# Top-2 expert layer in a fused six-layer kernel: first tile's rows picked on TensorE, last two tiles placed by TensorE

## The reference, cut to what matters

```python
x = x + _L1_attn_ref(_layernorm(x, axis=-1), ...)
x = x + _L1_ffn_ref(_layernorm(x, axis=-1), Wg, w1, w3, w2)

def _L1_ffn_ref(hidden_states, Wg, w1, w3, w2):      # 8 experts, top 2, hidden 256, inter 704
    router_logits = x @ Wg.T
    probs = jax.nn.softmax(router_logits, axis=-1)
    topk_vals, topk_idx = jax.lax.top_k(probs, TOP_K)
    topk_vals = topk_vals / jnp.sum(topk_vals, axis=-1, keepdims=True)
    combine = jnp.zeros((T, NUM_EXPERTS)).at[jnp.arange(T)[:, None], topk_idx].add(topk_vals)
    for e in range(NUM_EXPERTS):
        h = jax.nn.silu(x @ w1[e].T) * (x @ w3[e].T)
        out = out + combine[:, e:e + 1] * (h @ w2[e].T)
```

## Time and profile before

| what | value |
|---|---|
| median of 3 runs | 807.28 us |
| profiled execution, its own time | 807.86 us |
| profiled execution, span from first to last instruction | 806.0 us |
| TensorE busy | 737.7 us, 92% |
| VectorE busy | 563.9 us, 70% |
| ScalarE busy | 414.3 us, 51% |
| GpSimd busy | 310.5 us, 39% |
| largest entry of the chain that ended last | scatters into `sums_d`, 11% |
| mean granted TensorE clock | 0.91 |

### The profile page before, as it was taken

One profiled execution on the slowest core, in us unless ns is written; L12 is line 12 of the kernel. 1 busy time (PEld: TensorE's weight loads), 2 busy tenths in 40 slices (PEclk: granted clock), 3 DMA queues, 4 the chain that ended last, 5 costly groups with the idle time before them and its releaser, 6 DMA issues.

```text
span 806.0 us, 15830 instructions
## 1 busy us (share of the span) xinstructions
PE 737.7 (92%) x5985; PEld 585.5 (73%) x5985; DVE 563.9 (70%) x870; ACT 414.3 (51%) x892; POOL 310.5 (39%) x346
## 2 busy tenths in 40 slices
PE   7888999899999989979988899999889988999995
PEld 6623333678888767867865699986678865999995
DVE  5998997578887857777988566646588745655453
ACT  2877888335544434534455566653345540544542
POOL 2078888413332234433475113212133212232341
PEclk8855555799999999999999999999999999999999
DMA  6089999202211113311111011011011235999952
GB/s 191 26 147 160 173 167 181 66 14 78 75 61 57 44 39 93 91 53 38 48 55 52 14 34 53 28 47 66 27 54 41 86 119 193 395 390 380 325 136 69
DMA packets 110649, 87.92 MB, mean 109 GB/s; under 512 B 71313, under 2 KB 92177, under 8 KB 110578
## 3 DMA queue, kind: packets, MB, share of 16 engines
q1 hardware_dynamic: 107842, 83.16, 36.5%
q0 software_dynamic: 2736, 3.80, 2.5%
HBM read 66.62 MB, written 3.54 MB: 87 GB/s over the span
## 4 chain that ended last, share of the span: by engine, by line
PE 46%; DVE 17%; DMA 14%; POOL 9%; issue 7%; ACT 5%; DVEq 1%; SPq 0%; POOLq 0%; ACTq 0%
DMA sums_d<-og,scatter_idx 11%; PE ps L198 10%; PE ps L200 8%; PE ps L199 8%; POOL pt L856 6%; PE ps L1718 4%; PE ps L2101 2%; DVE x L1485 2%; PE ps L1188 2%; PE ps L1698 2%; DVE qrot L2273 2%; PE ps L2418 2%; POOL nb L863 2%; PE ps L1199 1%; ACT soft L2234 1%
## 5 line engine op out<-in xcount | busy, mean ns | idle before, releaser
L330 POOL TENSOR_TENSOR wa_lo<-raw,wa_hi 128x256 fp32r<-128x256 f32 (+1 forms) x76 | 85.6, 1131 | 184.9 <-ACT wa_hi L319 184.5
L330 POOL TENSOR_TENSOR wb_lo<-raw,wb_hi 128x256 fp32r<-128x256 f32 (+1 forms) x68 | 61.6, 911 | 129.4 <-ACT wb_hi L319 129.4
L959 ACT ACTIVATE kres<-ps,nb,qs 128x1024 int16<-128x1024 f32 x64 | 77.1, 1204 | 17.7 <-POOL nb L863 16.6
L2418 PE MATMUL ps<-xgt,tw 128*128 128x128 f32 x720 | 84.6, 278 | 1.4 <-ACT xgt L2484 1.4
L1092 DVE TENSOR_REDUCE nm<-ps 128x1 f32<-128x1024 f32 x64 | 78.0, 1222 | 9.8 <-PE ps L782 7.4
L2418 PEld LDWEIGHTS ps<-xgt,tw 128*128 128x128 f32 x720 | 83.2, 195 | 2.1 <-ACT xgt L2484 2.1
L198 PE MATMUL ps<-xt_hi,wa_hi 128*128 128x512 f32 (+1 forms) x168 | 68.5, 408 | 1.7 <-DVE soft L1343 0.9
L782 PE MATMUL ps<-qkt 48*128 48x512 bf16 x128 | 65.5, 617 | 4.9 <-ACT kres L959 3.8
L856 POOL CAST pt<-pti 128x1024 bf16<-128x1024 int16 x62 | 64.3, 1037 | 5.4 <-DMA pti<-kres 2.0
L199 PE MATMUL ps<-xt_lo,wa_hi 128*128 128x512 f32 (+1 forms) x168 | 65.0, 387 | 0.0
L200 PE MATMUL ps<-xt_hi,wa_lo 128*128 128x512 f32 (+1 forms) x168 | 64.9, 386 | 0.0
(11 more groups left out here) (414 smaller groups left out, 1941.7 us busy)
## 6 DMA issues: line engine op xcount, KB each, us to landing
tw<-w_l1f SPq DMA_DIRECT2D x15, 2304.0 KB, 13.9
raw<-w_l0a SPq DMA_DIRECT2D x16, 256.0 KB, 3.0
raw<-w_l1p SPq DMA_DIRECT2D x32, 128.0 KB, 2.1
raw<-w_l1x SPq DMA_DIRECT2D x32, 128.0 KB, 2.1
raw<-w_l1a SPq DMA_DIRECT2D x16, 256.0 KB, 2.6
raw<-w_l0f SPq DMA_DIRECT2D x12, 256.0 KB, 2.8
raw<-w_l0a SPq DMA_DIRECT2D x16, 128.0 KB, 2.1
wv_raw<-w_l0a SPq DMA_DIRECT2D x8, 256.0 KB, 3.2
```

Of the source, the lines that this page charges most:

```text
L330: last = nc.gpsimd.tensor_tensor(split_lo, src, split_hi.bitcast(F32), ALU.subtract)
L959: nc.scalar.activation(ei[:, n % RING, :], slot(n), ACT.Exp, bias=nb[:, n % 3:n % 3 + 1], scale=qs[:, col:col + 1], accum_out=sums[:, u, k ...
L2418: last = nc.tensor.matmul(up_gate(m, g)[:, k * P:(k + 1) * P], tw[:, slot_of_tile(m), k, (2 * g + c) * P:(2 * g + c + 1) * P], xgt[:, u, c ...
```

## The change

Three things are done in one edit.

1. **First tile.** Tile 0's rows are no longer gathered. VectorE builds `first_at`, a one-hot table of the tokens whose first-choice place (`own_i[:, 0:NT]`, the lower of a token's two places) lies in rows 0 to 127, and TensorE multiplies `xn` with it (8 float32 matmuls), which gives the transposed rows at once. The gathers are those of tiles 1 to 14, two of them before `scatter_idx` is awaited.
2. **Expert table.** `begun`, `begun_sum`, `expert_of` stand right after `first_at`, ahead of `own_tile`, `own_row` and the `place_j` tables. The weights by slot (`slot_weights`) are moved behind `up(0)` on TensorE and behind the first product on VectorE. Of the dummy matmuls twelve and two go, one is added.
3. **Last two tiles.** Tiles 13 and 14 are both placed by one-hot matmuls (8 tables `last_at`); their rows are split into `og_hi` (ScalarE) and `og_lo` (VectorE). The sums are loaded back after the scatter of tile 12. Tile 14's gate and product are made in two halves, and its down product is 6 float32 matmuls straight from `hx` and `tw` without the split.

```diff
+PLACED = TILES - 2
@@ tiles_sync
-            sp.wait_ge(added, 16 * LAST)
+            sp.wait_ge(added, 16 * PLACED)
@@ l1f_pe
             busy(pe, 2, 8)
+            pe.wait_ge(mo["first_at"], mo_at("first_at", 1))
+            for c in range(C2):
+                for t in range(NT):
+                    last = nc.tensor.matmul(ps[:, 4, c * P:(c + 1) * P], xn[:, t, c * P:(c + 1) * P], first_at[:, t, :], start=t == 0, stop=t == NT - 1)
+            last.then_inc(mo["x_t"], 1)
             pe.wait_ge(mo["token_v"], mo_at("token_v", 1))
...
-            busy(pe, 2, 12)
-            pe.wait_ge(mo["weight_v"], mo_at("weight_v", 1))
-            for j in range(8):
-                last = nc.tensor.matmul(ps[:, 7, 0:2 * SLOTS], place_j[:, j, :], weight_v[:, j, :], start=j == 0, stop=j == 7)
-            last.then_inc(mo["weights"], 1)
...
                         for c in range(C2):
                             last = nc.tensor.matmul(up_gate(m, g)[:, k * P:(k + 1) * P], tw[:, slot_of_tile(m), k, (2 * g + c) * P:(2 * g + c + 1) * P], xgt[:, u, c, :], start=c == 0, stop=c == 1)
+                        if m == LAST and g == 1 and k == 1:
+                            last.then_inc(mo["up"], 1)
...
-            gathered(0)
-            busy(pe, 2, 2)
+            busy(pe, 2, 1)
             for m in range(TILES + 1):
                 if m < TILES:
                     up(m)
+                if m == 0:
+                    slot_weights()
                 if m + 1 < TILES:
                     gathered(m + 1)
-                if m:
+                if m and m < TILES:
                     down(m - 1)
+            down_last(pe)
+            rows_placed(pe, PLACED)
+            rows_placed(pe, LAST)
+
+        def down_last(pe):
+            for i, k in enumerate((3, 4, 5, 0, 1, 2)):
+                if i % 3 == 0:
+                    pe.wait_ge(mo["h"], mo_at("h", TILES + i // 3))
+                last = nc.tensor.matmul(ps[:, 6, 0:D], hx[:, k * P:(k + 1) * P], tw[:, slot_of_tile(LAST), k, 4 * P:6 * P], start=i == 0, stop=i == CHUNKS - 1)
+            last.then_inc(mo["down"], 1)
@@ l1f_pool
-            for m in range(3):
+            for m in range(1, 3):
                 gather(m)
             pool.wait_ge(mo["scatter_at"], mo_at("scatter_at", 1))
-            for m in range(LAST + 2):
+            for m in range(PLACED + 2):
@@ l1f_act
-                h_high(m)
-                if m + 1 < TILES:
+                if m < LAST:
+                    h_high(m)
+                if m + 1 < LAST:
                     down_high(m + 1)
+            for m in (PLACED, LAST):
+                act.wait_ge(mo["down"], mo_at("down", m + 1))
+                nc.scalar.activation(og_hi[:, m - PLACED, :], ps[:, 7 if m < LAST else 6, 0:D], ACT.Copy, scale=slot_w[:, m:m + 1]).then_inc(mo["row_hi"], 1)
@@ l1f_dve
+            nc.vector.tensor_tensor(first_at[:], count_j[:].unsqueeze(1).broadcast_to([P, NT, P]), own_i[:, 0:NT].unsqueeze(2).broadcast_to([P, NT, P]), ALU.is_equal).then_inc(mo["first_at"], 1)
...
+                if m == LAST:
+                    dve.wait_ge(mo["up"], mo_at("up", TILES + 1))
+                    for k in range(2):
+                        cols = slice(3 * P * (1 - k), 3 * P * (2 - k))
+                        dve.wait_ge(mo["gate"], mo_at("gate", TILES + k))
+                        nc.vector.tensor_tensor(hx[:, cols], act_g[:, m % 2, cols], up_gate(m, 1)[:, cols], ALU.mult).then_inc(mo["h"], 1)
+                    return
...
+                if m >= PLACED:
+                    dve.wait_ge(mo["row_hi"], mo_at("row_hi", m - PLACED + 1))
+                    nc.vector.scalar_tensor_tensor(og_lo[:, m - PLACED, :], ps[:, 7 if m < LAST else 6, 0:D], slot_w[:, m:m + 1], og_hi[:, m - PLACED, :].bitcast(F32), ALU.mult, ALU.subtract).then_inc(mo["scaled"], 1)
+                    return
```

More of the change, by code:

```diff
@@ L549, in build @@
         masks = sb("masks", [P, 2, SLOTS], ctx=m5)
-        last_id = sb("last_id", [P, 1], ctx=m5)
-        last_at = sb("last_at", [P, NT, P], ctx=m5)
+        first_at = sb("first_at", [P, NT, P], ctx=m5)
+        last_id = sb("last_id", [P, 2], ctx=m5)
+        last_at = sb("last_at", [P, 2, NT, P], F32R, m5)
+        og_hi = sb("og_hi", [P, 2, D], F32R, m5)
+        og_lo = sb("og_lo", [P, 2, D], F32R, m5)
         logit = sb("logit", [P, NT, 16], ctx=m5)
@@ L2564, in l1f_dve @@
             dve.wait_ge(step, c.up())
+            nc.vector.tensor_tensor(first_at[:], count_j[:].unsqueeze(1).broadcast_to([P, NT, P]), own_i[:, 0:NT].unsqueeze(2).broadcast_to([P, NT, P]), ALU.is_equal).then_inc(mo["first_at"], 1)
+            dve.wait_ge(mo["ranks"], mo_at("ranks", 2))
+            dve.wait_ge(mo["table"], mo_at("table", 11))
+            nc.vector.tensor_tensor(begun[:], ps[:, 5, 0:8].unsqueeze(1).broadcast_to([P, SLOTS, 8]), tile_at[:].unsqueeze(2).broadcast_to([P, SLOTS, 8]), ALU.is_le).then_inc(step, 1)
+            dve.wait_ge(step, c.up())
+            nc.vector.tensor_reduce(begun_sum[:], begun[:], AX.X, ALU.add).then_inc(step, 1)
+            dve.wait_ge(step, c.up())
+            nc.vector.tensor_scalar(expert_of[:], begun_sum[:], -1.0, None, ALU.add).then_inc(mo["expert"], 1)
             nc.vector.tensor_scalar(own_tile[:], own_i[:], 7, None, ALU.arith_shift_right).then_inc(step, 1)
@@ L2578, in l1f_dve @@
             places(1)
[L2579 to L2585, removed]
             dve.wait_ge(mo["tokens"], mo_at("tokens", 1))
@@ L2646, in last_places, with slot_weights @@
                 dve.wait_ge(mo["scatter_at"], mo_at("scatter_at", 1))
-                nc.vector.tensor_copy(last_id[:], scatter_idx[:, LAST:TILES]).then_inc(step, 1)
+                nc.vector.tensor_copy(last_id[:], scatter_idx[:, PLACED:TILES]).then_inc(step, 1)
                 dve.wait_ge(step, c.up())
-                for t in range(NT):
-                    nc.vector.tensor_scalar(last_at[:, t, :], count_j[:], float(t * P), last_id[:, 0:1], ALU.add, ALU.is_equal).then_inc(mo["last_at"], 1)
+                for i in range(2):
+                    for t in range(NT):
+                        nc.vector.tensor_scalar(last_at[:, i, t, :], count_j[:], float(t * P), last_id[:, i:i + 1], ALU.add, ALU.is_equal).then_inc(mo["last_at"], 1)
+            def slot_weights():
+                dve.wait_ge(mo["weights"], mo_at("weights", 1))
+                nc.vector.tensor_copy(slot_w_lo[:], ps[:, 7, SLOTS:2 * SLOTS]).then_inc(step, 1)
+                dve.wait_ge(step, c.up())
+                nc.vector.tensor_tensor(slot_w[:], ps[:, 7, 0:SLOTS], slot_w_lo[:], ALU.add).then_inc(step, 1)
+                dve.wait_ge(step, c.up())
             down_low(0)
```

54 lines of the change are left out of this document (34 added, 20 removed).

## The result

| | before | changed |
|---|---|---|
| median, runs of one comparison | 809.53 us (15 runs, 805.01 to 813.45) | 803.29 us (15 runs, 799.44 to 809.14) |
| profiled execution, its own time | 807.86 us | 801.7 us |
| its span | 806.0 us | 799.9 us |

The ratio of the times is 0.9924, with a 95% interval from 0.9900 to 0.9949: 0.76% faster, some 6.1 us, and beyond the 0.5% that a measurement of this kernel can tell. The forecast was 0.53%. The absolute 803.0 us was met closely for a poor reason: the comparison ran some 2 us higher than the three runs of before that were known, so what has to be judged is the difference, 4.3 us foretold and 6.1 measured.

What follows compares the result with a forecast made beforehand. Bounds were taken to be when `up(1)` begins (tile 1's weights) and what follows `up(14)`. Span 806.0 - 0.4 (head) - 3.9 (tail) = 801.7, plus 1.86 is 803.6; against the median, 803.0 us, 0.53% faster, range 800.3 to 805.0.

Steps and rivals of the forecast that it cites:

- Routing and `up(0)`: Start of the kernel: `expert_of` ready 1.41 us earlier, load issued at 671.0, `up(0)` from about 672.65 to 678.2.
- Tile 1's landing: Load of tile 1's weights, which `up(1)` waits for: lands at 684.2 instead of 686.3, one gather less costing 0.7 us.
- The second rival: Tile 1's weights land early, at 681 to 682.5, up to 3.0 us more gain, 800.0 to 801.3 us; chance 0.09.
- the 683 that the prediction itself gave as a sign of being wrong: Start of `up(1)`: the prediction called itself wrong if this came before 683 or after 686.
- The clock: TensorE in `up(1)`: half clock after the pause ahead of it costs 1.8 us, range 1.5 to 2.2.
- The rival that the clock holds: TensorE keeps full clock through `up(1)`, saving the 1.8 us, 801.2 us in all; chance 0.14.
- Head: Stretch up to the end of `up(1)`: worth 0.4 us, ending at 691.6 against 692.07.
- Loads shared out: Rival: fourth load, issued at 678.3, shares bandwidth with tile 1's, which lands at 694.7; 813.5 us, slower; chance 0.05.
- The middle: Tiles between head and tail: only shift with the head, steady tiles staying at 7.65 us.
- Tail: From E, the end of `up(14)`: first add at E+6.6, end at E+10.6, a gain of 3.9 us, bounds 3.4 to 4.3.
- The sum: Whole kernel: span 806.0 less 0.4 for the head and 3.9 for the tail, 801.7 us.

Runs made afterwards that it cites:

- one gather more: Changed kernel plus one gather of tile 0's rows into an unread spare buffer, ahead of tile 1's gather but behind the load; 800.71 us.
- run with two transfers: Changed kernel with tile 1's weights loaded in two transfers, the up and gate part first, the down weights behind; 802.43 us.
- one piece: Changed kernel with tile 14's gate and product made whole instead of in two halves; 808.89 us.
- gathers 3 and 4 held: Changed kernel with the gathers of tiles 3 and 4 issued only after tile 1's rows are transposed; 803.62 us.
- table late: Changed kernel with the expert table back behind the place_j tables, so tile 1's load goes out behind the first gather; 810.94 us beside 807.92 for the kernel before.

## Where the prediction held and where it did not

- **Routing and `up(0)`.** `expert_of` 1.41 earlier, as foretold; the load issued at 671.46 for 671.0, which is the 0.46 of the earlier stages. `up(0)` from 672.95 for 672.65, in 5.52 us.
- **Tile 1's landing: the step that failed.** "One gather less lies in front: ... 0.7 each. So the landing is at 684.2", 13.2 us after issue; measured 10.7, at 682.15. The reason given was wrong with it: one gather more or two fewer behind the load left the landing at 9.9 and 10.5, not told apart from 10.7, and a gather in front of it made 14.0. I had taken the row of the same load "in the same company", and overlooked that the change also moved the load from 0.8 us behind the first gather to 1.9 ahead. Both could be read ahead of the result: that first gather goes out at 671.60 in the earlier trace rows, the load at 672.41 in the earlier trace rows. The second rival, that the load lands at 681 to 682.5 "since the load starts ahead of all gathers", is what happened, and it had 0.09. `up(1)` began at 682.29, ahead of the 683 that the prediction itself gave as a sign of being wrong.
- **The clock.** 1.8 foretold for the half clock, range 1.5 to 2.2; measured 1.6 (7.22 against 5.60), and the same in five experiments. In three others `up(1)` took 8.05, 8.14 and 8.44, which is 2.5 to 2.8 and outside of the range; there the clock was down before `up(1)` began. The stretch that was taken as 3.8 us at the half clock has a mean of 0.56 in the earlier trace rows, so about 3.3 us of it were at 0.50 (an estimate: 3.8 x 0.44 / 0.50); the cost of 1.73 was read from the passes and stands. The rival that the clock holds fell.
- **Head:** 0.4 foretold, 2.8 measured; the landing came 2.5 sooner than foretold after `own_i` (+13.6 against +16.1), the clock took 0.2 less, and some 0.2 were lost again between `up(1)` (3.0 ahead) and E (2.8 ahead).
- **Loads shared out.** The fourth load was issued at 678.9, before tile 1's landed; the loads still landed in order, at +13.6, +21.5, +27.5 and +34.2. That rival fell.
- **The middle.** Tile after tile at 7.67, with no gap, as said.
- **Tail:** E+6.6 to the first add foretold, 6.66 measured; 3.9 foretold, 3.8 measured. The sums' load went out at 789.03, so by the earlier trace rows (3.82) it was there at 792.9, 2.9 us ahead of the add; I had 2.8. The split by parts was not foretold well: unsplit product with its halves 2.6, the halves alone 0.4, and neither counts without the gate of the sums.
- **The sum.** 4.3 foretold, 6.1 measured. The head gave 2.4 more than foretold, nearly all by the landing, and the tail 0.1 less; the earlier stages, which ended 0.5 later in the profiled execution, take that much away.

**Still open.** Why a gather ahead of a load keeps it from completing. The Trainium skill, "DMA: Bandwidth & Descriptors", section "Why a DMA increments its semaphore by 16 and not by 1", says that a transfer runs on up to 16 engines which finish independently, and has landed with the last. The bytes fit with that: some engines could have gone on to the next loads while others were behind. Which engines, and whether the gather's descriptors hold them up, this profile does not show, and no run here tests it. The length of the half-clock stretch after one pause or another is not explained either, nor why tile 1's load took 11.7 us in one run and 9.9 in another at the same lead.

## What to carry to other kernels

When a step moves, write down its place relative to everything on the *other* queues, before and after, and take the duration only from a row with the same neighbours ahead of it. A large load that something waits for is worth trying ahead of the first indirect gather, and its part that is needed first in a transfer of its own. Dummy matmuls in the pause in front of a waiting burst gave back most of what the clock took (1.4 of 1.6 us), but look at the granted clock first: where it holds anyway, they are for nothing. At the end of a kernel, find the one wait that gates the tail before shortening the chain beside it.

## What was not expected of the hardware

- Moving one load from 0.6 us behind a gather to 3.0 us ahead of it cut its time to landing from 14.0 to 8.5 us at the same total rate (321 and 319 GB/s).
- The clock fell to 0.50 a microsecond into a burst that had already begun, after pauses of 0.66 and 1.91 us; eleven dummy matmuls in them kept it at 1.00. In the run with two transfers, with pauses of 0.85 and 0.47 us, it stayed at 1.00 without them.
- The loss did not simply grow with the pause: 2.94 us right ahead of `up(1)` (one piece) and 1.55 us (gathers 3 and 4 held) both gave 7.22, with the clock falling inside the burst, while 2.78 us ahead of the transposes (one gather more) gave 8.14 and 8.01 us (table late) 8.44, with the clock at 0.50 from the first pass on.
